# A router's norm one slot later, and ScalarE's projections ahead of its finishing work

## The reference

```python
x = x + mamba_like(layernorm(x))     # in_proj, conv of 4 taps, dt/B/C projections, scan, gate, out_w
x = x + moe(layernorm(x))            # router top 2 of 8 experts, plus one shared expert
# the scan, per channel (512) and state (16):
dA    = exp(clip(dt * A, -5, 5))     # dt = clip(sigmoid(u @ dt_w.T + dt_b), 1e-4, 1)
state = dA * state + dt * B * u + 1e-6
y     = sum(state * C, -1) + D * u   # then y * silu(z), @ out_w.T
# moe: combine = top-2 softmax weights; out = sum_e combine * down(silu(gate) * up) + sigmoid gate * shared
```

## Time and profile before

| | us |
|---|---|
| median of 3 runs (2903.06 to 2908.17) | 2906.48 |
| the profiled execution: time, span | 2905.48, 2903.7 |
| busy over the span: PE | 2524.9 (87%) |
| busy: DVE | 2238.2 (77%) |
| busy: ACT | 2031.3 (70%) |
| busy: POOL | 2234.9 (77%) |
| TensorE's mean granted clock | 0.952 |

### The profile page before, as it was taken

The page is one execution under the profiler, slowest core; times in us unless marked ns, Lnnn a source line. Parts: engine busy times, 40 slices in busy tenths (PEclk is TensorE's granted clock), DMA queues, the critical chain, the costliest instruction groups (busy, mean ns, idle before and its releaser), DMA issues. The chain is left out here.

```text
span 2903.7 us, 48476 instructions
## 1 busy us (share of the span) xinstructions
PE 2524.9 (87%) x15232; PEld 2206.8 (76%) x15232; DVE 2238.2 (77%) x4890; ACT 2031.3 (70%) x4675; POOL 2234.9 (77%) x1354
## 2 busy tenths in 40 slices
PE   7788888888888888888888888888886599999998
PEld 4777777777777777877777777777775488888887
DVE  2999999999999999999999999999998233333332
ACT  2888888888888888888888888888885133333332
POOL 1989999989999989999999999999996133333333
PEclk9899999999999999999999999999997799999999
DMA  4222222222222222222222222222220388888886
GB/s 173 74 76 86 81 78 78 85 78 78 97 90 81 77 81 92 78 81 89 77 78 84 79 77 80 93 92 81 74 90 28 118 201 202 200 200 200 203 201 153
DMA packets 138181, 309.62 MB, mean 107 GB/s; under 512 B 15040, under 2 KB 79680, under 8 KB 137792
## 3 DMA queue, kind: packets, MB, share of 16 engines
q1 hardware_dynamic: 110848, 270.03, 30.1%
q0 software_dynamic: 27072, 36.46, 6.2%
HBM read 258.42 MB, written 48.01 MB: 106 GB/s over the span
## 5 line engine op out<-in xcount | busy, mean ns | idle before, releaser
L1036 POOL TENSOR_TENSOR room<-dtu,b_all 128x1024 f32<-128x1024 f32 x512 | 1203.5, 2372 | 28.5 <-DVE dtu L1424 13.7
L798 ACT ACTIVATE room<-room,neg_a 128x256 f32<-128x256 f32 x2048 | 868.0, 497 | 0.8 <-DVE room L1213 0.8
L814 ACT ACTIVATE bank<-room,eps_col 128x512 f32<-128x512 f32 x1024 | 695.3, 683 | 238.1 <-DVE carry L1261 165.2
L600 PE MATMUL bank<-ident,room 128*128 128x128 f32 x4096 | 566.7, 287 | 193.2 <-POOL room L1025 107.6
L600 PEld LDWEIGHTS bank<-ident,room 128*128 128x128 f32 x4096 | 492.9, 148 | 256.4 <-POOL room L1025 117.4
L1247 DVE TENSOR_TENSOR_SCAN bank<-room,carry,bank 128x256 f32<-128x256 f32 x864 | 579.9, 735 | 55.7 <-ACT bank L814 55.5
L1025 POOL TENSOR_TENSOR room<-room,c_all 128x1024 f32<-128x1024 f32 x224 | 532.0, 2375 | 86.6 <-DVE bank L1247 58.6
L1161 POOL DMA_INDIRECT out<-room,ids x144 | 223.8, 1554 | 408.7 <-DMA out<-room,ids 182.9
L1326 DVE SCALAR_TENSOR_TENSOR hid<-hid,bank 128x256 f32<-128x256 f32 (+1 forms) x312 | 130.1, 417 | 420.2 <-ACT hid L909 420.2
L1247 DVE TENSOR_TENSOR_SCAN room<-room,carry,bank 128x256 f32<-128x256 f32 x672 | 446.0, 726 | 2.0 <-ACT bank L814 1.4
L552 PE MATMUL bank<-xnT,w_conv 128*128 128x256 f32 x3072 | 405.1, 288 | 7.0 <-ACT xnT L837 5.5
(11 more groups left out here) (150 smaller groups left out, 2962.5 us busy)
## 6 DMA issues: line engine op xcount, KB each, us to landing
b_all<-b_scratch SPq DMA_DIRECT2D x128, 512.0 KB, 4.0
c_all<-b_scratch SPq DMA_DIRECT2D x128, 512.0 KB, 5.3
room<-in_wgu SPq DMA_DIRECT2D x72, 704.0 KB, 5.8
room<-in_wd SPq DMA_DIRECT2D x72, 384.0 KB, 3.7
room<-x_by_expert SPq DMA_DIRECT2D x72, 260.0 KB, 2.9
x_in<-in_x SPq DMA_DIRECT2D x32, 256.0 KB, 6.2
x<-in_x SPq DMA_DIRECT2D x32, 256.0 KB, 2.7
out<-x SPq DMA_DIRECT2D x32, 256.0 KB, 4.2
```

Of the source, the lines that this page charges most:

```text
L600: last = mm(tr_bank[k][:, b * P:(b + 1) * P], v[n % VRING][:, b, k * P:(k + 1) * P], ident[:, :], is_transpose=True, start=False, stop=(n ...
L798: last = af(da[n % RING][:, b, :], dt[c.par][:, b, :], ACT.Exp, scale=neg_a[:, b, n:n + 1])
L814: af(v_slot(c, n, h)[:, :], v[n % VRING][:, 2 * h:2 * h + 2, :].rearrange("p b t -> p (b t)"), ACT.Identity, bias=eps_col[:, 0:1]).then_in ...
L1036: nc.gpsimd.tensor_tensor(out=v[n % VRING][:, :, :], in0=dtu[:, :, :], in1=row, op=ALU.mult) \
```

## The change

Three edits, all in the order of lists, none in the work itself:

1. PE: `post_norm` (four transposes) goes from ahead of `project` in slot 6 to behind it, so behind the first half of dt.
2. ACT: the second layernorm's two activations go from slot 5 to slot 6.
3. ACT: in each slot `norm_apply` (slot 4) and `project` go ahead of `finish`.

```diff
@@ PE, Body.__call__ @@
                         if post and slot == 3:
                             post_out(post)
-                        if post and slot == 6:
-                            post_norm(post)
                         if post and slot == 8:
                             post_route(post)
                         if post and slot == 10:
                             post_rank(post)
                         if proj:
                             project(proj, slot)
+                        if post and slot == 6:
+                            post_norm(post)
                         if norm and slot == 13:
                             proj_norm(norm)
@@ ACT, finish @@
-                if slot == 5:
+                if slot == 6:
                     act.wait_ge(o_rstd_ready, (c.index + 1) * RSTD_STEPS)
 
                     act.wait_ge(scat_done[c.par], c.pair * PICKS * NT * 16 + 16)
@@ ACT, Body.__call__ @@
                             add_eps(c, n, 1)
+                        if norm and slot == 4:
+                            norm_apply(norm)
+                        if proj:
+                            project(proj, slot)
                         if post:
                             finish(post, slot)
-                        if proj:
-                            project(proj, slot)
-                        if norm and slot == 4:
-                            norm_apply(norm)
                         if post:
                             for u in units_of(slot, GATE_SLOT):
                                 gate(post, u, False)
```

## The result

| | before | after |
|---|---|---|
| median, us (4 runs each) | 2906.74 (2903.06 to 2908.17) | 2838.37 (2837.71 to 2840.73) |
| ratio, 95% interval | | 0.977 (0.9754 to 0.9785) |
| profiled execution: time, span | 2905.48, 2903.7 | 2837.71, 2836.0 |
| TensorE's mean granted clock | 0.952 | 0.959 |

The kernel is 68 us faster, 23 us more than forecast. The waits that were to go went; the size of the gain did not hold.

A forecast was written before the change was run, and what follows sets the result against it. It took ACT's order in slots 5 to 8 to set POOL's and DVE's waits. 21.0 + 21.9 + 4 = 46.9, less two: 45 off 2905.48, so 2860.5, median 2861.5; likeliest range 2846 to 2880 (chance 0.61).

The forecast's parts named there:

- two loops: POOL's o_shift holds ACT, ACT holds PE and DVE, ACT's copy holds POOL; DVE's unbroken run delays ACT's bank. Gains priced on DVE's.
- The o_shift wait: ACT's norm moved to slot 6: 29.0 us of wait for POOL's o_shift, less 8.0 returning as waits for PE: 21.0.
- dt and b_row: ACT's waits in slots 5 to 8: 18.4 us for dt on the path and 3.5 of b_row, counted as gone: 21.9.
- the second half's wait: ACT's wait for dt's second half, 0.71 us each, 30 x 0.71 = 21.3, goes too but was counted at nothing.
- The rival "More": POOL falls to its limit, 97 us at the most; with the 0.71 waits counted, 45 + 21: 2840. Chance 0.06.
- z in slot 11: Tanh of z's second half passes two small activations (0.43 us); DVE waits 7.5 us for it, 4 taken.
- The rival "slower": PE's low clock moves into slots 1 to 4, conv ends 1.7 us later: 51 against 45, so 2912. Chance 0.09.
- The clock in slot 5: Low clock at PE's B and C should go with the shorter wait; if it stays, 11 to 13 us less gain.
- ACT's dt wait under 15: Sign: ACT's waits for dt, 39.7 us before, should be under 15 after the change.
- uT for the conv 6 to 8: Sign: a new wait of ACT's uT copy (L847) for PE's conv, some 6 to 8 us.
- POOL's wait for DVE at `c_times_state` from 58.6 to 25: Sign: POOL's wait for DVE's scan ahead of `c_times_state` falls from 58.6 us to about 25.
- DVE's down to 35: Sign: DVE's wait for ACT's `add_eps` falls from 77.5 us to about 35.

The follow-up runs named there:

- a late router: Full change plus eight spare transposes on PE ahead of slot 8's router matmuls: 2860.53 us; its pair, the full change with norm transposes done three times: 2859.45.

## Why the forecast was too small

**What bounds the kernel: open for the kernel before, right for the kernel after.** The prediction drew two loops, one by POOL's o_shift, ACT, PE and ACT's carry copy, and one through DVE, and priced everything by the second: "It is all on the loop through DVE". In the full change that holds: an earlier carry copy brought nothing, and four edits at DVE's steps moved the time. In the kernel before two gains of 8 us for DVE brought nothing, so there it fails or is hidden by the clock at B and C; the runs do not part the two.

**The o_shift wait: right.** 21.0 forecast; 29.0 less a new wait of uT for the conv, forecast at 8 and measured at 9.1 [after's waits], makes 19.9. That the norm alone brings 38 and not 21 is no contradiction: alone it also puts uT ahead of the norm, which is much of the second term.

**dt and b_row: right in what goes, short in what counts.** The step that failed is this one, of the second half's wait: "The second half's 0.71 goes as well, which brings ACT's copy and POOL on, but no `add_eps` that DVE waits for; I count it at nothing." It is true that no such `add_eps` gains by it, but the prediction stopped there. Two other things that DVE waits for stand behind PE's second half of dt: the router's matmuls, and so the top 2 in slot 9; and ACT's tanh of z, and so the z gate in slot 11. PE's order on top of the norm gave 7.3 and 5.3 us at these two places, and the full change has 6.4 and 5.6 there (the second without the edit in slots 10 and 11): 12 us where nothing was counted. That comparison also takes the first half's waits away, and PE being early and ACT's shorter wait come together in it; the one pair of kernels that parts these two, both with a late router, has 2.6 us at the z gate for ACT's wait. At the `add_eps` of slots 6 to 8 the term was nearly right: steps 6 to 9 gained 46.5 us, the sum had 42.9 less 2, about 41. The 5 us more are about what its waits give back beyond their length. The rival "More" had the total (2840 against 2838.4) by luck: its 21 us of second-half waits were 12, and other terms made up the rest.

**z in slot 11: 4 forecast.** By DVE's steps the edit in slots 10 and 11 is worth 5.2 us there, so the term was near. Taking it back costs 8.5 to 12 us in all, because it also costs 4.1 at step 4 to 5.

**Slot 4 to 5: nothing forecast, 5.7 measured.** It is mostly in position 0 (4.5 of it). There the change shortens TensorE's stretch at low clock in slots 0 and 1 from 24.3 to 15.6 us over seven bodies (worked out from the clock in the trace), and the full change pays 5 to 9 us for what is left. Why the stretch became shorter is not shown. The rival "slower" had this mechanism with its sign reversed: a low clock that moves into slots 1 to 4. It did not.

**Together.** Above the forecast's terms are 12 for the second half (6.4 at 9 to 10, 5.6 at 11 to 12), 5.6 at 6 to 9, 1.2 more for z, and 5.7 at 4 to 5: 24.5 us, where 23 were measured.

**The clock in slot 5: right.** B and C take 1.91 us, the window behind the shorter wait shows 1.00, and their mean over all bodies is 382 ns, which rules out the smaller gain. The rule of the Trainium skill that the prediction weighed (page "TensorE: Matmul & The Clock Gate", section "What's actually happening") would have the throttle released with activity; by it the low clock was to go, and the trace agrees. Its price is the less sure part: three quarters of it taken away in the kernel before gave 5 us, where the earlier trace rows made the whole 11 to 13.

**What the prediction said would show.** ACT's dt wait under 15: 0.9. uT for the conv 6 to 8: 9.1. POOL's wait for DVE at `c_times_state` from 58.6 to 25: 2.1 by that row; all its idle time there, 83.1, came down to 24.9. DVE's down to 35: 33.6, and 15.2 more at the scans into `room`, which it did not name (1.4 before). Bodies at 66 to 67: 66.2; position 3 at 65: 65.9. Nearly every sign came as forecast and the total still missed by a third: two places where DVE gained, steps 9 to 10 and 4 to 5, had no term in the sum.

## What to carry to other kernels

When several engines hold one another in a ring, a removed wait is worth its length only on the loop that binds. To find the loop, speed up one engine alone and look whether the time falls or a wait elsewhere grows; and look whether TensorE's clock stayed the same, since a longer idle time can lower it and take the gain away. Before a wait is put at nothing, follow it to everything behind it that the other engines take up, not only to the instruction that is waited for most: here the router's top 2 and the z gate stood behind it. Reorderings of lists must be priced together: here one edit was worth 0 alone and 47 us beside the other two, and a pair of them was worse than one.

## What was not expected of the hardware

- Spare matmuls in PE's idle time pay through the clock: 24 transposes in each of 7 bodies took the granted clock of slots 0 and 1 from 0.53 to 1.00 in the window above and gave 5 to 9 us on the full change and 16 to 20 with a late router; on the kernel before the same lines gave nothing, and the low clock came at B and C instead: 433 ns a matmul became 481.
- Activations on ACT that follow at once start 0.05 to 0.1 us before the end of the one before (1207.45 + 0.69 = 1208.14, the next at 1208.08). A removed wait gives its length and this overlap. On DVE, too, 45 waits fewer at steps 6 to 8 gave 0.1 us each beyond their length.
- The wait list can name a releaser that was long done. POOL's 58.6 us for DVE's scan in the earlier trace rows fell to 2.1 when ACT's carry copy came earlier, with the lists of DVE and POOL unchanged.
